# A two-layer graph network on one core: the constants are made and loaded in pieces between the first five turns

## The chip, the cores and the metric

The kernel runs on one core of one Trainium2 chip. The metric is the time of one execution on the device in microseconds (us). Times inside an execution come from one profiled run and count from the start of its span.

## The reference

64 graphs of 256 nodes with 256 features pass through two layers. Everything is computed in float32.

```
# layer 0
h = relu(layernorm(x));  A = adj + I;  d = rowsum(A) ** -0.5
x = x + relu((d A d) @ h @ W.T + b)
# layer 1, with the new x
h = relu(layernorm(x))
c = relu(bn1(conv1d(h, conv1_w, 1 tap)));  c = bn2(conv1d(c, conv2_w, 17 taps))
x_conv = relu(c + h)
s = h @ w_se.T + b_se;  D = exp(-|s_n - s_m|^2) * adj;  x_nmp = D @ relu(h @ w_msg.T + b_msg)
x = x + gru([x_conv, x_nmp], h)        # gates with w_ih, w_hh
```

bn(h) is h * g / sqrt(v + eps) + (b - m * g / sqrt(v + eps)). The scale of bn1 is multiplied into conv1_w, the scale of bn2 into the taps of conv2_w.

## The kernel before, in words

The program has three stages: the first runs over the 64 graphs (about 0 to 850 us), the second does the 17-tap convolution in the frequency domain, the third the gates. Only the start of the first stage is touched here.

The first stage is a software pipeline that is written out by hand. It has turns i = 0 to 71. In turn i every engine works on several graphs at once: graph i is loaded and its statistics are taken, graph i - 2 has its adjacency product (called AG here, with the graph's number), graph i - 3 its product with w0, graph i - 4 is transposed, graph i - 5 gets its products with wse and w1m, graph i - 6 its exponentials and graph i - 7 its Fourier transform and message product. Each engine has its own queue, with the functions first_sync, first_scalar, first_vector, first_gpsimd and first_tensor called for one turn after the other. Semaphores connect the queues, and an engine that waits holds up everything behind it in its queue. So turn 4 can be far along on DVE while TensorE is still at turn 3.

Each float32 product is done as three products of a high and a low part. ACT rounds the high part (names that end in h: ajh, hdxh, agh, w0h, w1mh, wseh), and DVE or GpSimd (POOL) subtracts it to get the low part (ajl, hdxl, agl, w0l, w1ml, wsel).

The constants: `ident` and `eye2` are unit matrices, `col` holds the per-channel vectors. From `col` DVE and GpSimd make `cold`, the scales and shifts of the two batch norms (with one power on GpSimd). DVE makes six diagonal matrices `diag` from it, TensorE multiplies them by ones so that each scale stands in a row in the banks CM1 and CM0 (the "rows"), ACT copies these to s1r, b1m and s2r. DVE multiplies st_w (the weights w1) by s1r, ACT and DVE split it in w1mh and w1ml. From s2r and the table tt_w DVE makes s2m and s2t, by which GpSimd scales the taps. `ft` and `gt` are the tables of the Fourier transforms.

In the kernel before, this whole chain stands on every engine between the calls for turn 3 and turn 4. ACT, GpSimd and DVE wait for its end before turn 4, and TensorE waits for s2r.

## Time and profile before

| | us |
|---|---|
| median of 3 runs | 1934.48 |
| lowest and highest | 1933.85, 1934.88 |
| the profiled execution, its own time | 1933.19 |
| its span | 1931.4 |
| TensorE busy | 1897.6 |
| DVE, ACT, GpSimd busy | 1118.9, 1029.9, 810.2 |

The profiled execution's own time is that of the whole program on the device; the span is the part that the trace shows. PE is TensorE, and PEld is its loading of weights. In a timeline row stand the start, the duration, the engine, the line of the kernel and the output and input names. In square brackets stands how long the engine was idle before it and what released it. Transfers are issued by the queue of SyncE (SP). Because matmuls overlap in the array, a row's duration is longer than the distance to the next row. The granted clock is given as a share of 2.4 GHz, so 0.50 is the level of 1.2 GHz.

### The profile page before, as it was taken

How to read it: one execution, taken by the hardware profiler on the slowest of the kernel's cores; microseconds unless marked ns; L12 is line 12 of the kernel's file. 1: busy time of each engine (PE TensorE's matmuls, PEld its weight loads, DVE VectorE, ACT ScalarE, POOL GpSimd, SP SyncE). 2: the span in 40 equal slices, each digit the busy share in tenths (PEclk: the TensorE clock that was granted, in tenths of full speed). 3: DMA queues.
4: the chain of work that ended last, by engine and by line, in shares of the span. 5: the costliest groups of instructions: out<-in, count | busy, mean ns of one | idle time of the engine just before them, and what ended most of it. 6: DMA issues, size and time to landing. Idle time of an engine off the chain costs nothing.

```text
span 1931.4 us, 29950 instructions
## 1 busy us (share of the span) xinstructions
PE 1897.6 (98%) x10524; PEld 1667.7 (86%) x10524; DVE 1118.9 (58%) x2187; ACT 1029.9 (53%) x1834; POOL 810.2 (42%) x1054
## 2 busy tenths in 40 slices
PE   4999999999999999999999999999999999999998
PEld 4899999999999989888888888888888888888887
DVE  6888989898887855444464344343344334434433
ACT  3888888888888875545563233233323323323322
POOL 4778888888776743333342122122122112212211
PEclk7999999999999999999999999999999999999999
DMA  5445655555455426556683322332232232233221
GB/s 170 158 169 177 212 189 195 180 193 200 171 201 182 148 99 157 143 138 163 147 224 108 115 91 92 104 108 84 95 115 86 86 115 86 87 114 97 87 96 55
DMA packets 254993, 262.58 MB, mean 136 GB/s; under 512 B 96519, under 2 KB 204423, under 8 KB 252798
## 3 DMA queue, kind: packets, MB, share of 16 engines
q1 hardware_dynamic: 254846, 260.68, 42.9%
q8 instruction: 85, 1.39, 0.3%
q14 instruction: 62, 0.51, 0.1%
HBM read 151.57 MB, written 109.05 MB: 135 GB/s over the span
## 4 chain that ended last, share of the span: by engine, by line
PE 96%; DVE 1%; ACT 1%; issue 1%; POOL 0%; DMA 0%; SPq 0%; DVEq 0%; POOLq 0%; ACTq 0%
PE P L104 77%; PE P L603 5%; PE P L872 5%; PE P L653 4%; PE P L632 3%; PE P L994 1%; PE P L624 1%; DMA yt<-y_d 0%; PE P L1265 0%; DVE ah L423 0%; DVE xxl L417 0%; POOL axl L534 0%; DVE wh0l L740 0%; DVE diag L1166 0%; ACT agh L344 0%
## 5 line engine op out<-in xcount | busy, mean ns | idle before, releaser
L856 POOL TENSOR_TENSOR xnx1l<-xnf,xnx1h 128x1024 fp32r<-128x1024 f32 x16 | 44.5, 2779 | 369.2 <-ACT xnx1h L849 369.2
L856 POOL TENSOR_TENSOR xnx0l<-xnf,xnx0h 128x1024 fp32r<-128x1024 f32 x15 | 41.6, 2773 | 340.4 <-ACT xnx0h L849 340.4
L967 DVE SCALAR_TENSOR_TENSOR gn<-tr,gn 128x512 f32<-128x512 f32 x64 | 44.3, 692 | 202.8 <-ACT tr L954 202.8
L954 ACT ACTIVATE tr<-P,cold 128x512 f32<-128x512 f32 x64 | 44.2, 690 | 217.1 <-PE P L104 217.1
L957 ACT ACTIVATE nn<-gn,col 128x512 f32<-128x512 f32 x64 | 46.3, 723 | 179.3 <-DVE gn L971 179.3
L534 POOL TENSOR_TENSOR axl<-af,axh 128x512 fp32r<-128x512 f32 x64 | 83.5, 1304 | 135.1 <-ACT axh L360 135.1
L961 ACT ACTIVATE tz<-P,cold 128x512 f32<-128x512 f32 x64 | 44.0, 688 | 164.0 <-PE P L104 164.0
L978 DVE SCALAR_TENSOR_TENSOR tz<-tz,tr 128x512 f32<-128x512 f32 x64 | 44.3, 692 | 149.7 <-ACT tz L961 149.7
L603 PE MATMUL P<-ft,h 128*128 128x240 f32 x512 | 114.3, 366 | 0.7 <-DVE x L444 0.7
L872 PEld LDWEIGHTS P<-gt,yt 128*128 128x128 f32 x768 | 108.3, 191 | 5.6 <-DMA yt<-y_d 0.8
L104 PE MATMUL P<-w1mh,xxh 128*128 128x512 f32 x256 | 112.1, 438 | 0.0
L872 PE MATMUL P<-gt,yt 128*128 128x128 f32 (+2 forms) x768 | 105.7, 287 | 0.2
L104 PE MATMUL P<-w1mh,xxl 128*128 128x512 f32 x256 | 101.2, 395 | 0.0
L104 PE MATMUL P<-w1ml,xxh 128*128 128x512 f32 x256 | 101.1, 395 | 0.0
L603 PEld LDWEIGHTS P<-ft,h 128*128 128x128 f32 x512 | 92.5, 190 | 5.8 <-issue 0.8
L971 DVE TENSOR_TENSOR gn<-gn,P 128x512 f32<-128x512 f32 x64 | 44.0, 688 | 86.7 <-PE P L104 86.6
L104 PE MATMUL P<-w0h,agh 128*128 128x256 f32 x256 | 85.2, 333 | 5.0 <-DVE w0l L1150 3.0
L104 PE MATMUL P<-ajh,hdxh 128*128 128x256 f32 x256 | 74.3, 290 | 14.5 <-DVE hdxl L402 12.4
L325 ACT ACTIVATE msh<-tcm 128x512 fp32r<-128x512 f32 x64 | 40.5, 632 | 89.5 <-PE P L104 88.7
L495 DVE TENSOR_TENSOR tcm<-P,b1m 128x512 f32<-128x512 f32 x64 | 44.2, 691 | 74.5 <-ACT h L382 74.5
L531 POOL TENSOR_TENSOR af<-af,at 128x512 f32<-128x512 f32 x64 | 82.2, 1284 | 7.3 <-ACT af L319 7.3
L539 POOL TENSOR_TENSOR ajl<-ah,ajh 128x512 fp32r<-128x512 f32 x64 | 82.2, 1285 | 2.0 <-ACT ajh L339 2.0
(219 smaller groups left out, 6710.0 us busy)
## 6 DMA issues: line engine op xcount, KB each, us to landing
xh_d<-xst SPq DMA_DIRECT2D x16, 1280.0 KB, 7.2
xl<-xh_d SPq DMA_DIRECT2D x40, 512.0 KB, 6.2
y_d<-yo SPq DMA_DIRECT2D x80, 256.0 KB, 2.4
x<-in_x SPq DMA_DIRECT2D x64, 256.0 KB, 3.0
a<-in_adj SPq DMA_DIRECT2D x64, 256.0 KB, 4.4
at<-in_adjt SPq DMA_DIRECT2D x64, 256.0 KB, 4.8
x_d<-x SPq DMA_DIRECT2D x64, 256.0 KB, 4.8
xn_d<-xt SPq DMA_DIRECT2D x64, 256.0 KB, 5.1
```

The source lines that it names most:

```text
L104: done = e.matmul(o, l, r, start=start, stop=stop, skip_group_check=True)
L531: e.e.tensor_tensor(af[:, :], af[:, :], at[b % 7][:, :], ALU.mult).then_inc(S["am"], 1)
L534: e.e.tensor_tensor(ax[1][:, :], af[:, :], ax[0][:, :], ALU.subtract).then_inc(S["axlo"], 1)
L539: e.e.tensor_tensor(ajl[b % 2][:, :], ah[:, :], ajh[b % 2][:, :], ALU.subtract).then_inc(S["ajlo"], 1)
L603: t = e.e.matmul(P[k][:, 0:3 * NT] if n == 0 else P[k][:, NT:4 * NT], h1[b % 2][:, n, c * 128:c * 128 + 128], ft[:, NT:4 * NT] if n == 0 e ...
L632: t = e.e.matmul(P[DIST][:, m * 256:m * 256 + 256], uv[0:96, 0, m * 128:m * 128 + 128], uv[0:96, 1, :], start=True, stop=True, skip_group_ ...
L653: t = e.e.matmul(P[k][:, m * 140:m * 140 + 140], taps[0:n_rows, j0 + m, c * 128:c * 128 + 128], tt_w[0:n_rows, part * 140:part * 140 + 140 ...
L856: e.e.tensor_tensor(o[1][:, :, :], xnf[p % 2][:, :, :, :].rearrange("p c i t -> p c (i t)"), o[0][:, :, :], ALU.subtract).then_inc(done, 1)
L872: t = e.e.matmul(P[k][:, o * 256 + first:o * 256 + last], y[:, j, o * 128:o * 128 + 128], gt[:, g:g + last - first], start=j == 0, stop=j ...
L957: e.e.activation(nn[:, :], gn[:, :], ACT.Tanh, bias=n_b[:, o:o + 1]).then_inc(S["nn"], 1)
L967: e.e.scalar_tensor_tensor(out=gn[:, :], in0=tr[:, :], scalar=1.0, in1=gn[:, :], op0=ALU.add, op1=ALU.mult).then_inc(S["v"], 1)
L978: e.e.scalar_tensor_tensor(out=tz[:, :], in0=tz[:, :], scalar=1.0, in1=tr[:, :], op0=ALU.add, op1=ALU.mult).then_inc(S["e"], 1)
```

## The change

The operations and the transfers are all kept. Their places in the queues change:

- SyncE: x, adj and the transposed adj of graph 0 come first, then eye2, col and ident, then x and adj of graph 1. tt_w is loaded after turn 4's loads, ft after turn 5's, gt after turn 20's.
- DVE: the first step of cold comes after turn 0; the rest of it and diag after turn 1; w0l and the scaling of st_w after turn 2; w1ml and wsel after turn 3; s2m, s2t and the two memsets of uv after turn 4.
- GpSimd: the power comes ahead of turn 0.
- TensorE: the rows' matmuls come after turn 2 (that is, behind AG0) and no longer after turn 3.
- ACT: w0h comes after turn 1, s1r and b1m after turn 2, w1mh, wseh and s2r after turn 3.
- The wait for all constants on ACT, GpSimd and DVE comes after turn 4, not after turn 3.

```diff
         def first_sync(e, i):
             if live(i, 0):
-                if i == 0:
-                    load_x(e, 0)
-                    load_adj(e, 0)
...
@@ sync
+            load_x(e, 0)
+            load_adj(e, 0)
+            load_adjt(e, 0)
+            sync.dma_start(eye2[:, :], eye).then_inc(S["eye2_in"], 16)
+            sync.dma_start(col[:, 0:29], cols).then_inc(S["col_in"], 16)
             sync.dma_start(ident[:, :], eye[:, 0:128]).then_inc(S["ident_in"], 16)
-            first_sync(e, 0)
-            sync.dma_start(col[:, 0:29], cols).then_inc(S["col_in"], 16)
-            sync.dma_start(eye2[:, :], eye).then_inc(S["eye2_in"], 16)
+            load_x(e, 1)
+            load_adj(e, 1)
             first_sync(e, 1)
...
             first_sync(e, 3)
+            first_sync(e, 4)
+            sync.dma_start(tt_w[:, :], ttab).then_inc(S["tt_in"], 16)
+            first_sync(e, 5)
             sync.dma_start(ft[:, :], ftab).then_inc(S["ft_in"], 16)
-            sync.dma_start(gt[:, :], gtab).then_inc(S["gt_in"], 16)
-            sync.dma_start(tt_w[:, :], ttab).then_inc(S["tt_in"], 16)
-            for i in range(4, TURNS):
+            for i in range(6, TURNS):
                 first_sync(e, i)
+                if i == 20:
+                    sync.dma_start(gt[:, :], gtab).then_inc(S["gt_in"], 16)
@@ scalar
-            for i in range(3):
+            for i in range(2):
                 first_scalar(e, i)
             e.wait_ge(S["w0_in"], 16)
             scalar.copy(w0[0][:, :, :], st_w0[:, :, :]).then_inc(S["chi"], 1)
-            first_scalar(e, 3)
+            first_scalar(e, 2)
             e.wait_ge(S["rows"], 1)
             scalar.copy(s1r[:, :], P[CM1][:, 0:256])
-            scalar.copy(b1m[:, 0:256], P[CM1][:, 256:512])
-            e.wait_ge(S["rows"], 2)
-            scalar.copy(s2r[:, 0:256], P[CM0][:, 0:256])
-            scalar.copy(s2r[:, 256:7 * NW], P[CM0][:, 0:7 * NW - 256]).then_inc(S["normrow"], 2)
+            scalar.copy(b1m[:, 0:256], P[CM1][:, 256:512]).then_inc(S["normrow"], 1)
+            first_scalar(e, 3)
             e.wait_ge(S["w1s"], 1)
             scalar.copy(w1m[0][:, :, :], st_w1[:, :, :]).then_inc(S["chi"], 1)
             e.wait_ge(S["se_in"], 16)
             scalar.copy(wse[0][:, :, :], st_se[:, :, :]).then_inc(S["chi"], 1)
+            e.wait_ge(S["rows"], 2)
+            scalar.copy(s2r[:, 0:256], P[CM0][:, 0:256])
+            scalar.copy(s2r[:, 256:7 * NW], P[CM0][:, 0:7 * NW - 256]).then_inc(S["normrow"], 1)
+            first_scalar(e, 4)
             e.wait_ge(S["clo"], 3)
             e.wait_ge(S["s2t"], 2)
-            for i in range(4, TURNS):
+            for i in range(5, TURNS):
                 first_scalar(e, i)
@@ gpsimd
-            for i in range(4):
-                first_gpsimd(e, i)
             e.wait_ge(S["consts"], 1)
             gpsimd.tensor_tensor(cold[:, 0:4], cold[:, 20:24], half[:, 0:4], ALU.pow).then_inc(S["crs"], 1)
+            for i in range(5):
+                first_gpsimd(e, i)
@@ tensor
-            for i in range(4):
+            for i in range(3):
                 first_tensor(e, i)
...
             t.then_inc(S["rows"], 1)
+            for i in range(3, 5):
+                first_tensor(e, i)
             e.wait_ge(S["normrow"], 2)
-            for i in range(4, TURNS):
+            for i in range(5, TURNS):
                 first_tensor(e, i)
```

Three places in the queues, as they stand in the program. First TensorE at turns 2 and 3, where the rows' matmuls (P<-diag,ones) now stand behind the last matmul of AG0 and ahead of the first product with w0:

```order
 L104 MATMUL P<-ajl_77,hdxh 128x256
 L104 MATMUL P<-ajh_75,hdxl 128x256
+L1275 MATMUL P<-diag,ones 128x128 [waits one,diag]
+L1275 MATMUL P<-diag,ones 128x128 x3
+L1279 MATMUL P<-diag,ones 128x128 x2
 L104 MATMUL P<-w0h,agh 128x256 [waits clo,aglo,aghi]
 L104 MATMUL P<-w0l,agh 128x256
```

The rows moved up by one turn; before, they stood behind AG1.

Second ACT at the start, where hd is the normalised graph and w0h a constant. Before:

```order
L374 ACTIVATE hd<-x_81,sm_100 128x256 [waits sbias]
L374 ACTIVATE hd<-x_81,sm_100 128x256
L307 CAST hdxh<-hd 128x512 [waits hd]
L339 CAST ajh_76<-ah 128x512 [waits ah]
L344 CAST agh<-P 128x512 [waits agg]
L374 ACTIVATE hd<-x_82,sm_101 128x256 [waits hdlo,sbias]
L374 ACTIVATE hd<-x_82,sm_101 128x256
L1088 CAST w0h<-st_w_122 128x512 [waits w0_in]
```

And now:

```order
L371 ACTIVATE hd<-x_81,sm_100 128x256 [waits sbias]
L371 ACTIVATE hd<-x_81,sm_100 128x256
L1092 CAST w0h<-st_w_122 128x512 [waits w0_in]
L304 CAST hdxh<-hd 128x512 [waits hd]
L336 CAST ajh_76<-ah 128x512 [waits ah]
L341 CAST agh<-P 128x512 [waits agg]
```

The copy w0h, which waits for the load of w0, moved ahead of hdxh of graph 0.

Third ACT between turns 3 and 4, behind hd of graph 2, as it is now:

```order
L371 ACTIVATE hd<-x_83,sm_102 128x256 [waits hdlo,sbias]
L371 ACTIVATE hd<-x_83,sm_102 128x256
L1099 CAST w1mh<-st_w_123 128x1024 [waits w1s]
L1101 CAST wseh<-st_se 128x256 [waits se_in]
L1103 COPY s2r<-P 128x256 [waits rows]
L1104 COPY s2r<-P 128x3
L304 CAST hdxh<-hd 128x512 [waits hd]
```

Before, s1r and b1m stood here too, and hdxh waited for all of the constants (its row had [waits hd,s2t,clo]).

## Rows read from the trace of the kernel before

**Rows 1.** The page: busy time of TensorE, and its chain.

```profile
PE 1897.6 (98%) x10524; PEld 1667.7 (86%) x10524; DVE 1118.9 (58%) x2187; ACT 1029.9 (53%) x1834; POOL 810.2 (42%) x1054
PE 96%; DVE 1%; ACT 1%; issue 1%; POOL 0%; DMA 0%; SPq 0%; DVEq 0%; POOLq 0%; ACTq 0%
```

**Rows 2.** Windows: stretch, length, busy us (instructions) by engine, clock, DMA, GB/s.

```profile
24.00:29.00 5.00, 0.00 (x0) 0.00 (x0) 3.56 (x20) 1.18 (x3) 1.01 (x1) 0.76 0.69 211
29.00:47.00 18.00, 13.79 (x59) 12.86 (x60) 13.90 (x34) 9.22 (x19) 7.80 (x19) 0.50 0.20 58
48.00:66.00 18.00, 17.45 (x117) 15.49 (x115) 15.24 (x39) 16.34 (x32) 12.50 (x22) 1.00 0.46 148
66.00:850.00 784.00, 782.04 (x5008) 718.14 (x5009) 614.22 (x1379) 625.07 (x1211) 536.25 (x839) 1.00 0.54 173
```

**Rows 3.** Timeline of TensorE in the first 50 us.

```profile
12.40 0.55 PE L104 MATMUL P<-ajh,hdxh 128*128 128x256 f32 x1 [12.40 <-DVE hdxl L402]
...
14.89 0.41 PE L104 MATMUL P<-ajh,hdxl 128*128 128x256 f32 x1
18.30 0.55 PE L104 MATMUL P<-w0h,agh 128*128 128x256 f32 x1 [2.99 <-DVE w0l L1150]
...
23.29 0.28 PE L104 MATMUL P<-ajh,hdxl 128*128 128x256 f32 x1
29.16 2.08 PE L1265 MATMUL P<-diag,ones 128*128 128x128 f32 x8 [5.59 <-DVE diag L1166]
31.02 1.06 PE L1269 MATMUL P<-diag,ones 128*128 128x128 f32 x4
...
45.52 0.41 PE L104 MATMUL P<-ajh,hdxh 128*128 128x256 f32 x1
```

**Rows 4.** Timeline of DVE in the first 53 us.

```profile
11.57 0.73 DVE L402 TENSOR_TENSOR hdxl<-hd,hdxh 128x512 fp32r<-128x512 f32 x1
...
25.49 0.36 DVE L394 BATCH_NORM_AGGREGATE sm<-sm 128x2 f32<-128x6 f32 x4
...
27.84 1.26 DVE L1166 TENSOR_SCALAR diag<-ident,cold 128x128 f32<-128x128 f32 x6
...
33.27 0.42 DVE L1174 TENSOR_TENSOR s2m<-s2r,tt_w 119x259 f32<-119x259 f32 x1
...
36.80 0.69 DVE L402 TENSOR_TENSOR hdxl<-hd,hdxh 128x512 fp32r<-128x512 f32 x1
...
40.16 1.29 DVE L454 TENSOR_SCALAR sm<-sm 128x2 f32<-128x2 f32 x1
...
43.58 0.66 DVE L402 TENSOR_TENSOR hdxl<-hd,hdxh 128x512 fp32r<-128x512 f32 x1
...
52.93 0.69 DVE L402 TENSOR_TENSOR hdxl<-hd,hdxh 128x512 fp32r<-128x512 f32 x1 [2.25 <-ACT hdxh L307]
```

**Rows 5.** SyncE's queue: the issue of w0's load; then loads, us to landing.

```profile
6.53 0.47 SPq L1030 DMA_DIRECT2D st_w<-in_w0t x1
...
st_w<-in_w0t SPq DMA_DIRECT2D x1, 256.0 KB, 5.2
st_w<-in_w1mt SPq DMA_DIRECT2D x1, 512.0 KB, 6.2
```

**Rows 6.** Timeline of ACT in the first 35 us.

```profile
16.82 0.61 ACT L1088 CAST w0h<-st_w 128x512 fp32r<-128x512 f32 x1
...
24.09 1.09 ACT L374 ACTIVATE hd<-x,sm 128x256 f32<-128x256 f32 x2
...
33.39 1.04 ACT L1097 CAST w1mh<-st_w 128x1024 fp32r<-128x1024 f32 x1 [0.83 <-DVE st_w L1171]
```

**Rows 7.** Timeline of GpSimd between turns 3 and 4.

```profile
25.99 1.01 POOL L1236 TENSOR_TENSOR cold<-cold,half 128x4 f32<-128x4 f32 x1 [4.63 <-DVE cold L1153]
```

**Rows 8.** The chain that ended last: start, length, what.

```profile
42.82 5.02 PE P L104 x24
...
72.06 4.97 PE P L104 x42
```

More of the change, by code:

```diff
@@ L1146, in _ @@
             e = Engine(vector)
-            for i in range(3):
-                first_vector(e, i)
-            e.wait_ge(S["chi"], 1)
-            vector.tensor_tensor(w0[1][:, :, :], st_w0[:, :, :], w0[0][:, :, :], ALU.subtract).then_inc(S["clo"], 1)
-            first_vector(e, 3)
+            first_vector(e, 0)
             e.wait_ge(S["col_in"], 16)
             vector.tensor_scalar(cold[:, 20:24], col[:, 12:16], EPS, None, ALU.add).then_inc(S["consts"], 1)
+            first_vector(e, 1)
             e.wait_ge(S["crs"], 1)
@@ L1160, in _ @@
             vector.tensor_tensor(cold[:, 8:12], col[:, 16:20], col[:, 22:26], ALU.add).then_inc(S["consts"], 1)
+            e.wait_ge(S["ident_in"], 16)
             e.wait_ge(S["consts"], 5)
-            vector.tensor_scalar(cold[:, 8:12], cold[:, 8:12], 0.5, None, ALU.mult)
-            vector.tensor_scalar(cold[:, 12:14], col[:, 26:28], 0.5, None, ALU.mult)
-            e.wait_ge(S["ident_in"], 16)
             for n, k in enumerate((0, 1, 4, 5, 2, 3)):
@@ L1167, in _ @@
             t.then_inc(S["diag"], 1)
-            e.wait_ge(S["normrow"], 2)
+            vector.tensor_scalar(cold[:, 8:12], cold[:, 8:12], 0.5, None, ALU.mult)
+            vector.tensor_scalar(cold[:, 12:14], col[:, 26:28], 0.5, None, ALU.mult)
+            first_vector(e, 2)
+            e.wait_ge(S["chi"], 1)
+            vector.tensor_tensor(w0[1][:, :, :], st_w0[:, :, :], w0[0][:, :, :], ALU.subtract).then_inc(S["clo"], 1)
+            e.wait_ge(S["normrow"], 1)
             e.wait_ge(S["w1_in"], 16)
@@ L1172, in _ @@
             t.then_inc(S["w1s"], 1)
+            first_vector(e, 3)
+            e.wait_ge(S["chi"], 2)
+            vector.tensor_tensor(w1m[1][:, :, :], st_w1[:, :, :], w1m[0][:, :, :], ALU.subtract).then_inc(S["clo"], 1)
+            e.wait_ge(S["chi"], 3)
+            vector.tensor_tensor(wse[1][:, :, :], st_se[:, :, :], wse[0][:, :, :], ALU.subtract).then_inc(S["clo"], 1)
+            first_vector(e, 4)
+            e.wait_ge(S["normrow"], 2)
             e.wait_ge(S["tt_in"], 16)
@@ L1177, in _ @@
             vector.tensor_reduce(s2t[:, :], s2m[:, :, :], AX_X, ALU.add).then_inc(S["s2t"], 1)
-            e.wait_ge(S["chi"], 2)
-            vector.tensor_tensor(w1m[1][:, :, :], st_w1[:, :, :], w1m[0][:, :, :], ALU.subtract).then_inc(S["clo"], 1)
-            e.wait_ge(S["chi"], 3)
-            vector.tensor_tensor(wse[1][:, :, :], st_se[:, :, :], wse[0][:, :, :], ALU.subtract).then_inc(S["clo"], 1)
             e.wait_ge(S["clo"], 3)
@@ L1232, in _ @@
             e.wait_ge(S["half"], 1)
-            for i in range(4):
-                first_gpsimd(e, i)
             e.wait_ge(S["consts"], 1)
             gpsimd.tensor_tensor(cold[:, 0:4], cold[:, 20:24], half[:, 0:4], ALU.pow).then_inc(S["crs"], 1)
+            for i in range(5):
+                first_gpsimd(e, i)
             e.wait_ge(S["clo"], 3)
             e.wait_ge(S["s2t"], 2)
-            for i in range(4, TURNS):
+            for i in range(5, TURNS):
                 first_gpsimd(e, i)
@@ L1271, in _ @@
             t.then_inc(S["rows"], 1)
+            for i in range(3, 5):
+                first_tensor(e, i)
             e.wait_ge(S["normrow"], 2)
-            for i in range(4, TURNS):
+            for i in range(5, TURNS):
                 first_tensor(e, i)
```

## The prediction

> **What bounds the kernel now.** I read the page first. TensorE is busy for 98% of the span, and 96% of the chain that ended last is TensorE's [rows 1]. So only what makes TensorE wait, or run slowly, can move the time. The windows say where that is: from 66 to 850 us it is busy for 782.04 of 784 us, from 24 to 29 us for 0.00 of 5, and from 29 to 47 us for 13.79 of 18 with a granted clock of 0.50, which is the 1.2 GHz level [rows 2]. The constants are made in just that stretch.
>
> The start of TensorE's timeline shows the same. The first group of 12 matmuls (the adjacency product of graph 0, "AG0") begins at 12.40 and ends near 15.3. The first product with w0 begins at 18.30 after 2.99 us of idle time, released by w0l. The last matmul of AG1 begins at 23.29. Then come 5.59 us of nothing until diag is there at 29.16, and AG3 begins only at 45.52 [rows 3]. On DVE the normal work of turn 3 ends at 25.8 and that of turn 4 begins at 36.80. The 11.0 us between hold the chain cold, diag, rows, s1r, w1mh, w1ml, and every queue waits for its end [rows 4]. DVE then begins turn 5 at 43.58 and turn 6 at 52.93 [rows 4]. I use these starts as checkpoints: how much earlier does each come after the change? Once TensorE has no gaps, a lead is kept to the end, since the clock stands at 1.00 and nearly nothing waits from 66 us on [rows 2].
>
> **The change, part by part.** No instruction is added or removed, so the sum is made of waits.
>
> (1) *The head, a loss of 1.3 us.* On ACT the copy w0h now stands ahead of hdxh of graph 0. It waits for the w0 load, issued at 6.53 and 5.2 us on its way, so there at 11.7 [rows 5]. The same loads (nine of 256 KB, cols and ident) are asked for ahead of it in either order, so I leave 11.7. Then w0h takes 0.61 [rows 6], hdxh about as much, ready near 12.9, and from hdxl's start to AG0's it was 0.83 (11.57 to 12.40, [rows 3, 4]). AG0 begins at 13.7 instead of 12.40. The bounds are 0 (the copy fits before hd is ready) and 2 us (the load lands 0.7 later).
> The power on GpSimd, 1.01 us [rows 7], now runs ahead of graph 0's statistics, but needs only the cols load; it delays hd by little, as hd stood behind ajh before. DVE makes cold and diag (2.1 us, from the end of the power at 27.0 to the last diag near 29.1, [rows 4, 7]) while it would wait for hdxh. Both costs lie under the w0 wait.
>
> (2) *The rows' matmuls, no cost.* They take 2.9 us (29.16 to 32.08, [rows 3]) and stand between AG0 and the first w0 product, where TensorE idled 2.99 us. AG0 ends at 16.6, the rows at 19.5. The w0 product begins there instead of at 18.30: 1.2 us late. Without the gap they would cost 2.9.
>
> (3) *Turn 3.* Everything follows the w0 product by the same distances as before, so DVE's last row of turn 3 ends at 27.0, or 26.3 if only AG1's own end counts; I take 26.7 (before 25.8). The st_w product and s1r's copies are done while AG1's inputs are late anyway.
>
> (4) *From turn 3 to turn 5, the gain.* ACT's hd of graph 2 began at 24.09 and took 1.0 [rows 6]; 0.9 later it ends at 26.0, and w1mh (1.04) at 27.05. So DVE waits 0.35 us where 11.0 stood. The rest of the constants' DVE work stays: from 33.27 to 36.80 it took 3.5 us [rows 4], now split in w1ml and wsel ahead of turn 4 and s2m, s2t and the memsets behind it. ACT's wseh and s2r are smaller than w1mh, together 0.9 at most, so with them hdxh is begun by 28.0 and ready near 28.5, when DVE is through w1ml and wsel (a little under half of the 3.5, so near 28.6). They cost nothing, but only just. Turn 4 itself took 43.58 - 36.80 = 6.8. Turn 5 begins at 26.7 + 0.35 + 3.5 + 6.8 = 37.4 instead of 43.58: a lead of 6.2. Of turn 4's time 1.1 went to a single tiny operation of DVE that took 1.29 at 40.16 [rows 4]; without it the lead is 7.3. I take 6.8.
>
> (5) *Turn 5 and the clock.* In the kernel before, the clock was 0.50 until 47 us [rows 2]. From DVE's start of turn 5 to AG3's it was 1.94 us (43.58 to 45.52), as the product ahead still ran at the low level. With only hdxl in the way it is 0.83, so 1.1 less. At the high level 42 matmuls of 256 columns take 4.97, or 0.118 each; at the low one 24 take 5.02 from 42.82 on, or 0.209 each [rows 8]. AG3 at the high level is then up to 0.9 shorter (12 x 0.09 is 1.1, but its last part had the high level before). Together 2.0, and DVE's idle time ahead of turn 6, 2.25 us with hdxh to blame [rows 4], is there to be saved. So if the clock is up in turn 5, the lead grows by 1.1 to 2.0, I take 1.6: 6.8 + 1.6 = 8.4. If it is down all through it, the six small and twelve 512-column matmuls that had the high level before cost 6 x 0.09 = 0.5 and 12 x 0.18 = 2.2 more, and AG3 0.2: 2.9 less the 1.1 is a loss of 1.8, and nearer 0 if the clock rises halfway.
>
> The clock came back only when TensorE had worked without a gap from 42.82 to 47 us [rows 8], and was lost in the gap of 5.59 us: the window from 24 to 29 us, all of it idle, has 0.76 on average, so the fall comes well inside the idle stretch [rows 2, 3]. After the change no single gap is that long. The longest I find are about 2 us, ahead of AG2 and of the next two products, with TensorE busy for somewhat under half of the time between 25 and 36 us. I take it that the clock rises during AG1 as before and stays.
> The Trainium skill speaks against this: "TensorE: Matmul & The Clock Gate", section "A second HAM failure mode: psum-queue depth-cycling", has TensorE idling briefly but often between groups of matmuls, and its clock going up and down from that. By that rule the gain would be that of the low clock below, 6.0 us; no run here yet shows which holds.
>
> (6) *The loads.* x1 and a1 now come behind eye2, cols and ident: some 0.4 MB more ahead of them, about 1 us at the pace of this stretch, hidden by DVE's other work. tt_w is issued only after a load that waits for x2 of graph 0 (near 24.7), so at 26.6, and needs 6.2 us if it is as slow as the slowest load of that time [rows 5]: there at 32.8, wanted by DVE near 34. ft is wanted only in turn 7, gt after the first stage. Nothing is lost, with 1 us to spare for tt_w.
>
> **The sum.** -8.4 us against the profiled execution's own 1933.19 (its span is 1931.4) gives 1924.8. The median of the runs is 1934.48, 1.3 above it, so the forecast is 1926.1.
>
> **The rivals.**
> *A, the clock falls between turns 3 and 5.* For it: TensorE works less than half of that time. Against it: the only fall in the trace came in one long gap. Lead 6.8 plus between -1.8 (low all through turn 5) and +0.2 (up again right behind AG3, so that only AG3 and the small ones pay), so -0.8: 6.0 us gained, 1928.5; down to 6.2 - 1.8 = 4.4 with the smaller lead, 1930.1.
> *B, the pieces land on queues that were not idle.* DVE and ACT are busy 13.90 and 9.22 us of the 18 from 29 to 47 us. If w1mh, wseh and s2r hold up hdxh, and with it AG2, agh and the next product, by their full 1.9 us, the head costs 2 instead of 1.3, and the clock is low too, then 4.4 - 1.9 - 0.7 = 1.8 us are left: 1932.7, within 0.2%. That asks for three things at once.
> *C, slower: the late tt_w load.* DVE's s2m waits for it, and s2t holds all of turn 5 on ACT, GpSimd and DVE. Each us beyond 34 costs one. It decides if the load takes over 8.4 + 7.4 = 15.8 us from its issue; at 20 us the kernel would take 1938.7. The slowest early load took 6.2 [rows 5], which speaks against it.
> *D, more than forecast.* w0 lands before hd is ready (0.6 less loss), no slow operation (7.3) and the full 2.0: 9.9, or 1924.6; up to 11, or 1923.5, if the turns also lose small waits.
>
> **How the numbers follow.** Forecast (clock stays up) 0.52, A 0.28, B 0.08, C 0.03, D 0.09. The range takes in the forecast, A with its smaller lead, and D: 1923.5 to 1930.4, which leaves about 0.14 out. 0.2% is 3.9 us, about what a measurement of this kernel can tell from no change. Forecast, A and D gain more: 0.88 with a hundredth off for overlap. B, with the small end of A, is the same: 0.09. C: 0.03.
>
> **What would show it.** In the changed kernel's profile: AG0 near 13.7, released behind w0h; the rows' matmuls straight behind AG0 with no gap ahead of the w0 product; DVE's turn 4 starting near 28.6, turn 5 near 36.8 and turn 6 near 44.5 (before 36.80, 43.58, 52.93); granted clock 1.00 between 25 and 45 us. A clock of 0.50 in turn 5 shows A; DVE waiting ahead of s2m for a DMA shows C; ACT's w1mh beginning after 27 us, or hdxh of graph 2 after 29, shows B. From turn 7 on both kernels should need the same time for a turn; if they don't, the prediction is wrong in its ground.

## The result, and the profile after

| | median us | lowest to highest, runs |
|---|---|---|
| before | 1934.16 | 1932.19 to 1934.88, 4 |
| changed | 1922.36 | 1921.82 to 1923.34, 4 |

The ratio is 0.9941, with a 95% interval of 0.9924 to 0.9958. The change gains 11.8 us. The forecast was 8.4, so 1926.1, with a range that began at 1923.5. The time lies 1.1 us below it. The profiled execution took 1921.82 us, with a span of 1920.0. When the same kernel was measured once more with the last experiments (the run *again*), it had 1923.75 (1922.47 to 1924.92, 5 runs) beside 1933.6 for the kernel before (1932.58 to 1935.41, 9 runs), which is 9.85 gained. That median would lie just inside the forecast's range, so a median of a few runs is good to about 1 us here, and the 1.1 us alone prove little. The traces are clearer: both profiled executions of the changed kernel have more than the 8.4 us of the forecast (11.9 and 11.0 us at the first Fourier product), and the part that failed can be named.

The page of the changed kernel, busy time and the chain that ended last (compare [rows 1]):

```profile
PE 1890.4 (98%) x10524; PEld 1660.9 (87%) x10524; DVE 1117.7 (58%) x2187; ACT 1029.5 (54%) x1834; POOL 811.3 (42%) x1054
PE 97%; DVE 1%; ACT 1%; issue 1%; DMA 0%; POOL 0%; SPq 0%; DVEq 0%; POOLq 0%; ACTq 0%
```

TensorE still bounds the kernel, with the same 10524 matmuls. They are busy for 7.2 us less, as fewer of them run at the low level.

The windows of the changed kernel, with the columns and stretches of [rows 2]:

```profile
24.00:29.00 5.00, 3.31 (x24) 2.96 (x24) 5.00 (x15) 2.52 (x8) 3.67 (x7) 1.00 0.75 244
29.00:47.00 18.00, 14.78 (x96) 13.21 (x97) 17.00 (x48) 15.12 (x30) 11.99 (x27) 1.00 0.51 162
48.00:66.00 18.00, 17.43 (x121) 16.31 (x121) 16.60 (x42) 15.24 (x30) 15.13 (x26) 1.00 0.51 167
66.00:850.00 784.00, 782.13 (x4998) 717.51 (x4997) 609.29 (x1362) 622.47 (x1203) 529.77 (x826) 1.00 0.54 173
```

Where TensorE did nothing from 24 to 29 us it now does 24 matmuls, and from 29 to 47 us it does 96 and not 59, at the high level. DVE, busy for only 58% of the span, is the one to look at: 5.00 of 5 us and 17.00 of 18. While the pipeline fills, DVE sets the pace and TensorE has time to spare.

TensorE's timeline of the changed kernel, as [rows 3]:

```profile
13.54 0.55 PE L104 MATMUL P<-ajh,hdxh 128*128 128x256 f32 x1 [13.54 <-DVE hdxl L399]
...
16.02 0.41 PE L104 MATMUL P<-ajh,hdxl 128*128 128x256 f32 x1
16.24 1.27 PE L1275 MATMUL P<-diag,ones 128*128 128x128 f32 x8
17.35 0.61 PE L1279 MATMUL P<-diag,ones 128*128 128x128 f32 x4
18.66 0.36 PE L104 MATMUL P<-w0h,agh 128*128 128x256 f32 x1 [0.70 <-DVE w0l L1174]
18.86 0.28 PE L104 MATMUL P<-w0l,agh 128*128 128x256 f32 x1
18.97 0.28 PE L104 MATMUL P<-w0h,agl 128*128 128x256 f32 x1
...
24.18 0.36 PE L104 MATMUL P<-w0h,agh 128*128 128x256 f32 x1 [2.43 <-DVE agl L470]
...
31.42 0.35 PE L104 MATMUL P<-w0h,agh 128*128 128x256 f32 x1 [1.69 <-DVE agl L470]
...
34.51 0.36 PE L104 MATMUL P<-ajh,hdxh 128*128 128x256 f32 x1 [1.45 <-ACT hdxh L304]
...
54.18 1.86 PE L600 MATMUL P<-ft,h 128*128 128x240 f32 x8 [0.57 <-DVE x L441]
```

The rows' matmuls stand behind AG0 without a gap, as forecast. But they take 1.7 us and not the 2.9 of [rows 3]: the last four take 0.61 where four took 1.06. The first w0 product then runs with 0.12 us from start to start, the high level, where AG0 ran with 0.21. The clock rose early in the rows' matmuls, near 16.5 us (an estimate: from 16.24 the first eight take 1.11 us up to the next row; they took 1.86 at the low level, and 0.99 in c_both below, all at the high one). The first Fourier product begins at 54.18; before it was 66.10. That is a lead of 11.9 us, of which 11.4 are left in the span. From turn 8 (60.45 for 72.37) to turn 65 (670.86 for 682.64) on DVE the lead goes from 11.92 to 11.78 us, so both kernels need the same time per turn within 0.01 us; the other 0.4 goes behind that, where the change touches nothing.

The kernel was profiled a second time (again), and there the clock rose later:

```profile
16.93 1.91 PE L1275 MATMUL P<-diag,ones 128*128 128x128 f32 x8
18.64 1.06 PE L1279 MATMUL P<-diag,ones 128*128 128x128 f32 x4
19.36 0.55 PE L104 MATMUL P<-w0h,agh 128*128 128x256 f32 x1
...
20.35 0.28 PE L104 MATMUL P<-w0l,agh 128*128 128x256 f32 x1
```

All the rows' matmuls ran at the low level here, and the high one came near 20.3 us, inside the first w0 product. What that product's start has to do with the level is taken up in step 2 below.

DVE's timeline of the changed kernel, as [rows 4]:

```profile
10.22 2.28 DVE L1168 TENSOR_SCALAR diag<-ident,cold 128x128 f32<-128x128 f32 x6
...
12.74 0.69 DVE L399 TENSOR_TENSOR hdxl<-hd,hdxh 128x512 fp32r<-128x512 f32 x1
...
19.30 0.68 DVE L399 TENSOR_TENSOR hdxl<-hd,hdxh 128x512 fp32r<-128x512 f32 x1
...
24.66 0.36 DVE L391 BATCH_NORM_AGGREGATE sm<-sm 128x2 f32<-128x6 f32 x4
24.93 1.19 DVE L1182 TENSOR_TENSOR w1ml<-st_w,w1mh 128x1024 fp32r<-128x1024 f32 x1
26.04 0.42 DVE L1184 TENSOR_TENSOR wsel<-st_se,wseh 128x256 fp32r<-128x256 f32 x1
26.38 0.69 DVE L399 TENSOR_TENSOR hdxl<-hd,hdxh 128x512 fp32r<-128x512 f32 x1
...
29.81 0.16 DVE L452 TENSOR_SCALAR sm<-sm 128x2 f32<-128x2 f32 x1
29.88 0.68 DVE L458 SCALAR_TENSOR_TENSOR x<-x,x 128x512 f32<-128x512 f32 x1
...
32.02 0.40 DVE L1188 TENSOR_TENSOR s2m<-s2r,tt_w 119x259 f32<-119x259 f32 x1
...
33.72 0.69 DVE L399 TENSOR_TENSOR hdxl<-hd,hdxh 128x512 fp32r<-128x512 f32 x1
...
41.30 0.69 DVE L399 TENSOR_TENSOR hdxl<-hd,hdxh 128x512 fp32r<-128x512 f32 x1 [0.56 <-ACT hdxh L304]
...
50.10 0.69 DVE L399 TENSOR_TENSOR hdxl<-hd,hdxh 128x512 fp32r<-128x512 f32 x1 [0.34 <-ACT hdxh L304]
```

Each hdxl begins a turn. None of these rows from 12.74 to 33.72 has a wait in brackets, the pieces of the constants included. Against [rows 4] turn 4 begins 10.4 us earlier (26.38 for 36.80), turn 5 9.9 (33.72 for 43.58), turn 6 11.6 (41.30 for 52.93) and turn 7 11.9 (50.10 for 62.02).

ACT's timeline of the changed kernel, as [rows 6]:

```profile
10.59 1.09 ACT L371 ACTIVATE hd<-x,sm 128x256 f32<-128x256 f32 x2 [2.54 <-POOL sm L523]
11.59 0.60 ACT L1092 CAST w0h<-st_w 128x512 fp32r<-128x512 f32 x1
12.10 0.61 ACT L304 CAST hdxh<-hd 128x512 fp32r<-128x512 f32 x1
...
23.26 1.03 ACT L1099 CAST w1mh<-st_w 128x1024 fp32r<-128x1024 f32 x1
```

And GpSimd's, as [rows 7]:

```profile
6.95 1.33 POOL L1244 TENSOR_TENSOR cold<-cold,half 128x4 f32<-128x4 f32 x1 [5.91 <-DVE cold L1156]
...
29.90 0.71 POOL L523 TENSOR_TENSOR sm<-sm 128x2 f32<-128x2 f32 x1
30.58 1.27 POOL L536 TENSOR_TENSOR ajl<-ah,ajh 128x512 fp32r<-128x512 f32 x1
```

At the head the queue was held in another place than forecast. hd waited for GpSimd, which first waited for cold and then ran the power: the statistics of graph 0 began behind it at 8.25 us. w0h then ran without a wait for its load, and hdxl stood behind diag. This differs between executions of the same kernel: in again hd began at 10.80, and w0h at 12.28 after 0.39 us of waiting for its load, and hdxl then waited 0.60 us for hdxh.

### The profile page after: what moved, and what is told of

The parts are those of the page before. It is cut to its first block, busy times and chain, and to the rows that moved or that the text cites. A ratio compares the mean times of both kernels' runs of the same rounds, so it can differ in the third digit from the quotient of the medians.

```text
span 1920.0 us, 29952 instructions
## 1 busy us (share of the span) xinstructions
PE 1890.4 (98%) x10524; PEld 1660.9 (87%) x10524; DVE 1117.7 (58%) x2187; ACT 1029.5 (54%) x1834; POOL 811.3 (42%) x1054
## 4 chain that ended last, share of the span: by engine, by line
PE 97%; DVE 1%; ACT 1%; issue 1%; DMA 0%; POOL 0%; SPq 0%; DVEq 0%; POOLq 0%; ACTq 0%
PE P L104 77%; PE P L600 5%; PE P L869 5%; PE P L650 4%; PE P L629 3%; PE P L991 2%; PE P L621 1%; DMA col<-in_cols 0%; ACT hd L371 0%; DMA yt<-y_d 0%; DVE x L441 0%; ACT hdxh L304 0%; DVE sm L430 0%; DVE ah L420 0%; DVE hdxl L399 0%
```

## The experiments

The checkpoints are those above: the start of AG0, the turns on DVE, and the first Fourier product. The experiments ran in three groups. The kernel before, measured in each group, had 1933.02 (25 runs), 1933.01 (9) and 1933.6 (9). Ratios are to it. Where AG0 begins is not exact to a tenth: the four profiled kernels with the head of the kernel before (before, c_gap, c_hole, c_both) have 12.40, 13.13, 12.64 and 12.15, and the five with the head of the changed one (changed, again, late, x_act, x_dve) have 13.54, 14.24, 14.04, 14.17 and 13.92.

**First group: what the clock is worth, and what the long wait is worth.** Three kernels take the kernel before and only keep TensorE busy. The extra products go to a bank that is overwritten later. *c_gap* fills the idle stretch behind AG0, as the rows' matmuls do in the changed kernel:

```diff
-            for i in range(4):
+            for i in range(3):
                 first_tensor(e, i)
+            e.wait_ge(S["one"], 1)
+            for n in range(6):
+                tensor.matmul(P[DFT][:, 0:128], ones[:, :], ones[:, :], start=True, stop=True, skip_group_check=True)
+            first_tensor(e, 3)
```

> The kernel before, with six extra 128x128 float32 matmuls of ones in TensorE's idle time between AG0 and the first w0 product (into a bank that nothing uses yet). My theory now: in the changed kernel the rows' matmuls fill this gap, the clock therefore rises near 17 us instead of 23, and turn 3 ends 1.8 us early from that. Then here too the matmuls of the w0 product stand about 0.12 us apart, DVE's last row of turn 3 ends near 24.2 instead of 25.8, and the kernel takes 1.5 to 2 us less than the kernel before. Rival: the early rise comes from something else (the phase of whatever the chip looks at); then the clock still rises near 23 us and the time is that of the kernel before, within 0.5 us.

*c_hole* fills the 5.59 us behind AG1 in which the clock fell:

```diff
             for i in range(4):
                 first_tensor(e, i)
+            for n in range(44):
+                tensor.matmul(P[DFT][:, 0:256], w0[0][:, 0, 0:128], w0[0][:, 0, :], start=True, stop=True, skip_group_check=True)
```

> The kernel before, with 44 extra 128x256 matmuls behind AG1, 5.2 us of work in the idle time of 5.6 us ahead of the rows. The chain of constants is untouched. Theory: the clock then stays up from 23 us on, which saves about 1.3 us on the rows, little in turn 4 (DVE and ACT set its pace), and about 2 in turn 5: 3 to 4 us less than the kernel before, so the clock is about a third of the 11.8 us and the stall of the queues the rest. Rival: the gain of the change is mostly the clock; then this kernel gains 7 us or more.

*c_both* has both edits.

> The kernel before with both fillers, so that TensorE's clock is up from 17 us on and the chain of constants stands where it stood. Theory: the two gains add, 5 to 6 us less than the kernel before, and 6 us stay for the move of the chain itself. Rival (clock is nearly all): 10 us or more.

| | median us (range, runs) | ratio (95%) | first Fourier product |
|---|---|---|---|
| c_gap | 1930.94 (1929.56 to 1932.93, 10) | 0.999 (0.998 to 0.9999) | 62.98 |
| c_hole | 1931.40 (1930.23 to 1932.35, 10) | 0.9991 (0.9981 to 1.0001) | 63.43 |
| c_both | 1930.37 (1928.58 to 1931.94, 10) | 0.9986 (0.9977 to 0.9996) | 62.62 |

The first w0 product on TensorE in c_gap:

```profile
19.02 0.36 PE L104 MATMUL P<-w0h,agh 128*128 128x256 f32 x1 [1.58 <-DVE w0l L1150]
19.22 0.28 PE L104 MATMUL P<-w0l,agh 128*128 128x256 f32 x1
19.34 0.28 PE L104 MATMUL P<-w0h,agl 128*128 128x256 f32 x1
```

And the last row of turn 3 on DVE in c_gap:

```profile
24.21 0.37 DVE L394 BATCH_NORM_AGGREGATE sm<-sm 128x2 f32<-128x6 f32 x4
```

Six small matmuls in the gap bring the w0 product and AG1 to 0.12 us from start to start. Turn 3, from its hdxl at 18.79 to this row, takes 5.42 us. In the kernel before it took 7.42 (18.07 to 25.49). In the changed kernel it takes 5.36 (19.30 to 24.66). In c_hole, with no filler in the gap, turn 3 and the chain behind it keep their length: 10.95 us from hdxl to the rows' matmuls, before 11.09, c_gap and c_both 9.09. So the early clock alone is enough for the 2 us of turn 3. It takes them out of two waits, which DVE has in turn 3 of the kernel before and in c_gap no more:

```profile
21.24 0.88 DVE L444 SCALAR_TENSOR_TENSOR x<-P,sm,b 128x256 f32<-128x256 f32 x2 [1.22 <-PE P L104]
...
24.22 0.69 DVE L473 TENSOR_TENSOR agl<-P,agh 128x512 fp32r<-128x512 f32 x1 [0.65 <-ACT agh L344]
```

In the changed kernel the clock had help. There the first w0 product begins 0.64 us before turn 3's hdxl (18.66 and 19.30), before it began 0.23 behind it (18.30 and 18.07), so DVE would have waited less at either level. An estimate: with the distances of the kernel before from the w0 product on (2.94 us to x, 5.92 to agl), DVE would have waited 0.4 us at x and 0.75 at agl. So some 1.2 of the 2 us are the clock there, and 0.9 the earlier product. In again, where the clock rose only near 20.3 us, turn 3 took the same 5.36 us, with the product 0.88 us ahead of hdxl. No run took the clock's rise out of the changed kernel, so this division is not shown.

The second thing that the group tells is a limit. Both fillers together gained 2.65 us, and I had expected about twice that; c_hole gained 1.6 for an expected 3 to 4, and its interval still takes in no gain at all. One window of c_both shows why:

```profile
29.00:47.00 18.00, 13.09 (x68) 12.13 (x69) 17.11 (x44) 10.79 (x22) 10.44 (x24) 0.72 0.28 87
```

The clock fell again, in the 3.31 us in which TensorE waited for hdxh of turn 4, and turn 5 was slow once more (9.37 us from hdxl to hdxl, before 9.35). In c_hole it fell in turn 4 too (0.60 from 36 to 40 us), behind a wait as long. By c_hole and c_gap, in which the clock was back in time, turn 5 is 7.95 and 7.85 long.

The lead of 11.9 us that the changed kernel has on DVE at turn 7 can now be added up. Turn 3 is 2.1 us shorter, turn 4 1.1 (the slow operation of [rows 4] is not there), turn 5 1.8 and turn 6 0.3. The long wait behind turn 3 went from 11.31 us (25.49 to 36.80) to 1.72 (24.66 to 26.38), with 1.70 more behind turn 4, so it gives 7.9. The later hdxl of turn 3 (19.30 for 18.07) takes 1.2 back. Of the 7.9, the high level alone gives back 1.2: from hdxl of turn 3 to that of turn 4 it is 16.73 us in c_gap and 15.51 in c_both. The rest, near 6.7, came back in none of the kernels in which only the clock was helped.

**Is it the place of the pieces, or only that they are pieces?** *late* takes the changed kernel and moves the pieces between turns 3 and 4 behind turn 4, on ACT and DVE:

```diff
 @@ scalar, behind first_scalar(e, 3)
+            first_scalar(e, 4)
             e.wait_ge(S["w1s"], 1)
             scalar.copy(w1m[0][:, :, :], st_w1[:, :, :]).then_inc(S["chi"], 1)
...
             scalar.copy(s2r[:, 256:7 * NW], P[CM0][:, 0:7 * NW - 256]).then_inc(S["normrow"], 1)
-            first_scalar(e, 4)
 @@ vector, behind first_vector(e, 3)
+            first_vector(e, 4)
             e.wait_ge(S["chi"], 2)
             vector.tensor_tensor(w1m[1][:, :, :], st_w1[:, :, :], w1m[0][:, :, :], ALU.subtract).then_inc(S["clo"], 1)
...
-            first_vector(e, 4)
```

> The changed kernel, with w1mh, wseh, s2r (ACT) and w1ml, wsel (DVE) moved from behind turn 3 to behind turn 4, together with s2m and s2t. Theory: between 25 and 41 us DVE is busy nearly all the time, so the place of its constants in the queue matters little and their sum counts: the time is that of the changed kernel, 0 to 1.5 us more, since now ACT's 1.6 us and DVE's 3.2 us come one behind the other with DVE waiting for w1mh. DVE's turn 4 starts 1.5 us earlier, its turn 5 0 to 1.5 later. Rival: the spreading over several turns is what gains; then a block in one place costs 3 us or more.

Measured 1925.56 (1923.90 to 1926.67, 4 runs), ratio 0.9962 (0.9947 to 0.9977), first Fourier product 56.66. The Fourier product is 2.5 us behind that of the changed kernel and 1.5 behind that of again; late gains 7.5 us over the kernel before beside it, where the changed kernel gained 9.9 and 11.8, and its profiled execution is the fastest of its four. It falls between the two expectations. The wait that I had overlooked stands on TensorE, in the row of late where turn 5 begins with its product with w0:

```profile
33.67 0.58 PE L104 MATMUL P<-w0h,agh 128*128 128x256 f32 x1 [3.78 <-ACT s2r L1105]
34.05 0.42 PE L104 MATMUL P<-w0l,agh 128*128 128x256 f32 x1
```

TensorE waits for both copies to be out of the banks before turn 5, and the copy s2r came late; 3.78 us of idle time also cost the high level (0.21 from start to start behind it). So some of the long wait comes back if these pieces are put in one place, even one turn later, and the place counts for some 1.5 to 4 us.

**Second group: the head.** Three kernels try to take away the 1.1 us (1.8 in again) by which AG0 is late. *v1* puts w0h behind hdxh of graph 0. *v2* puts GpSimd's power behind the statistics of turns 0 and 1, and DVE's cold and diag behind hdxl of graph 0. *v3* does both. The function given as third argument is called right behind hdxh or hdxl; round_w0 and make_diag hold the lines that are taken out.

```diff
 @@ v1, scalar
-            e.wait_ge(S["w0_in"], 16)
-            scalar.copy(w0[0][:, :, :], st_w0[:, :, :]).then_inc(S["chi"], 1)
-            first_scalar(e, 2)
+            first_scalar(e, 2, round_w0)
 @@ v2, gpsimd
+            for i in range(2):
+                first_gpsimd(e, i)
             e.wait_ge(S["consts"], 1)
             gpsimd.tensor_tensor(cold[:, 0:4], cold[:, 20:24], half[:, 0:4], ALU.pow).then_inc(S["crs"], 1)
-            for i in range(5):
+            for i in range(2, 5):
                 first_gpsimd(e, i)
 @@ v2, vector
-            e.wait_ge(S["crs"], 1)
-            vector.tensor_tensor(cold[:, 0:4], cold[:, 0:4], col[:, 0:4], ALU.mult).then_inc(S["consts"], 1)
...
-            first_vector(e, 2)
+            first_vector(e, 2, make_diag)
```

> The changed kernel with the copy w0h put behind hdxh of graph 0 (ahead of ajh of graph 1). Theory: in the changed kernel's trace hd of graph 0 waits 2.54 us for GpSimd and w0h runs right behind it without waiting for its load, so w0h costs only its own 0.5 us; but DVE is busy with diag till 12.6, so hdxl cannot start before that and the time stays the same within 0.3 us. Rival (my prediction): the w0 load sets AG0's start; then AG0 begins at 12.9 or earlier and the kernel gains 0.6 to 1.2 us.

> The changed kernel with the power on GpSimd put behind turn 1 (behind graph 0's statistics and ajl) and DVE's cold and diag put behind hdxl of graph 0. Theory: graph 0's statistics are 1.3 us earlier, hd starts near 8.3 instead of 10.59, DVE is free for hdxl; w0h still stands ahead of hdxh and its load lands near 11.4, so now the load does set the start: AG0 near 13.2 instead of 13.54, the kernel 0 to 0.5 us faster.

> Both moves together: hd near 8.3, hdxh near 9.3, hdxl near 10, AG0 near 10.8 instead of 13.54. Theory: nothing else holds AG0, and the loads of graph 1 come in time, so the kernel is 2 to 2.7 us faster than the changed kernel, 13.8 to 14.5 faster than the kernel before. Rival: the loads (x, adj of graphs 1 to 3, w0) set the pace of turns 2 and 3; then the lead at AG0 is given back by AG1 and the time is that of the changed kernel within 0.5 us.

*u_sp* is the changed kernel with the loads in the order of the kernel before:

```diff
-            load_x(e, 0)
-            load_adj(e, 0)
-            load_adjt(e, 0)
-            sync.dma_start(eye2[:, :], eye).then_inc(S["eye2_in"], 16)
-            sync.dma_start(col[:, 0:29], cols).then_inc(S["col_in"], 16)
             sync.dma_start(ident[:, :], eye[:, 0:128]).then_inc(S["ident_in"], 16)
+            load_x(e, 0)
+            load_adj(e, 0)
             load_x(e, 1)
             load_adj(e, 1)
+            load_adjt(e, 0)
+            sync.dma_start(col[:, 0:29], cols).then_inc(S["col_in"], 16)
+            sync.dma_start(eye2[:, :], eye).then_inc(S["eye2_in"], 16)
```

> The changed kernel with the load order of the kernel before (ident first, cols and eye2 behind graph 1's loads, ft, gt and tt_w behind turn 3's). Theory: cols then lands near 7.7 instead of 6.6, so the power, graph 0's statistics behind it and hd are 1.1 us later, eye2 lands near 8.5 and ah with it: AG0 near 14.7, the kernel 1 to 1.3 us slower than the changed kernel. The late tables make no difference. Rival: the load order is worth nothing (the w0 load lands at the same time in both); then AG0 stays at 13.5 and the time is the same.

| | median us (range, 5 runs) | ratio (95%) | AG0 | first Fourier product |
|---|---|---|---|---|
| v1 | 1922.19 (1921.06 to 1922.32) | 0.9943 (0.993 to 0.9955) | 13.86 | 54.64 |
| v2 | 1922.74 (1921.91 to 1923.38) | 0.9947 (0.9935 to 0.996) | 13.76 | 55.18 |
| v3 | 1920.39 (1919.05 to 1923.78) | 0.9937 (0.9924 to 0.9951) | 11.45 | 53.22 |
| u_sp | 1923.24 (1922.88 to 1923.48) | 0.9949 (0.9937 to 0.9962) | 15.05 | 55.93 |

Neither v1 nor v2 alone moves AG0 out of the 13.54 to 14.24 us that the same head has elsewhere: it is held in two places, and each takes over when the other is gone. In v1 GpSimd's power still holds hd; in v2 w0h now waits for its load and holds hdxh (hdxl at 12.96 after 2.84 us of idle time, released by hdxh). Both edits together bring AG0 to 11.45, 2.1 us earlier than in the changed kernel and 2.8 earlier than in again. But only 1.0 and 1.9 us of it reach the first Fourier product. DVE has hardly any idle time from 10.65 on in v3 (3.89, 4.00, 3.97 and 4.00 us busy in the four stretches of 4 us from 12 on), and diag, which has left the stretch ahead of hdxl, now stands behind it (12.07 to 13.3). A head that is earlier is paid back by the engine that sets the pace. In this execution the clock fell as well. TensorE's timeline of v3:

```profile
22.99 0.36 PE L104 MATMUL P<-w0h,agh 128*128 128x256 f32 x1 [2.26 <-DVE agl L472]
...
23.65 0.41 PE L104 MATMUL P<-w0h,agl 128*128 128x256 f32 x1
23.86 0.42 PE L104 MATMUL P<-w0h,agh 128*128 128x256 f32 x1
```

From 23.65 on a matmul of 256 columns stands 0.21 us from the next. The granted clock is 0.50 from 24 to 28 us and 0.69 to 32. Turn 4's and turn 5's DVE times hardly show it (7.58 us each; the changed kernel has 7.34 and 7.58), because TensorE does not set the pace there.

u_sp shows what the new order of the loads does. With the old order AG0 comes 1.2 to 1.5 us later than in v1 and the changed kernel (0.8 later than in again), and the time is 1.05 us longer than that of v1 and 0.5 longer than that of v2 beside it. It is the constants' loads that matter: DVE's first step of cold waits for cols until 8.36, where it was 6.62, and GpSimd's power and all behind it move with it. From hdxl of turn 3 to that of turn 5 u_sp takes 14.43 us, the changed kernel 14.42. The loads act on the head alone.

**Third group: which engine sets the pace.** *x_dve* puts one more subtraction of 1024 columns ahead of w1ml on DVE, *x_act* one more copy of 1024 columns ahead of w1mh on ACT. Both write to xst, a buffer that is filled later:

```diff
 @@ x_dve, vector
             e.wait_ge(S["chi"], 2)
+            vector.tensor_tensor(xst[0][:, 0, 0:64, :].rearrange("p r t -> p (r t)"), st_w1[:, :, :].rearrange("p k n -> p (k n)"), w1m[0][:, :, :].rearrange("p k n -> p (k n)"), ALU.subtract)
             vector.tensor_tensor(w1m[1][:, :, :], st_w1[:, :, :], w1m[0][:, :, :], ALU.subtract).then_inc(S["clo"], 1)
 @@ x_act, scalar
             e.wait_ge(S["w1s"], 1)
+            scalar.copy(xst[0][:, 0, 0:64, :].rearrange("p r t -> p (r t)"), st_w1[:, :, :].rearrange("p k n -> p (k n)"))
             scalar.copy(w1m[0][:, :, :], st_w1[:, :, :]).then_inc(S["chi"], 1)
```

> The changed kernel with one more DVE subtraction of 128x1024 (some 1.2 us) ahead of w1ml, into a tile that nothing uses yet. Theory: from hdxl of graph 0 on DVE has no idle time until turn 6, and its queue sets the pace of turns 3 to 5, so 1.0 to 1.2 us come out at the end: turn 4 starts near 27.6 instead of 26.38, and the kernel is 1.0 to 1.2 us slower than the changed kernel of the same job. Rival: TensorE's waits or ACT set the pace; then 0 to 0.3.

> The changed kernel with one more ACT copy of 128x1024 (1.0 us) ahead of w1mh. Theory: ACT had w1mh ready 0.75 us before DVE came to it, and hdxh of graph 2 1.0 us before, so of the 1.0 us only 0.2 to 0.3 come out. Rival (B of the prediction: the pieces on ACT hold up hdxh and with it everything): 1.0 us.

*again* is the changed kernel itself, as the measure for this group:

> The changed kernel itself, for the three above to stand against on the same chip: 1922.4 within 0.5 us, 11 to 12 us less than the kernel before.

*v4* is v3 with the wait for the constants in turn 5 moved behind hdxh on ACT and, with the two memsets of uv, behind hdxl on DVE:

```diff
 @@ scalar
-            e.wait_ge(S["clo"], 3)
-            e.wait_ge(S["s2t"], 2)
-            for i in range(5, TURNS):
+            first_scalar(e, 5, constants_done)
+            for i in range(6, TURNS):
 @@ vector
-            e.wait_ge(S["clo"], 3)
-            e.wait_ge(S["s2t"], 2)
-            vector.memset(uv[32:64, 0, :], -0.5)
-            vector.memset(uv[64:96, 1, :], -0.5).then_inc(S["ones"], 1)
-            for i in range(5, TURNS):
+            first_vector(e, 5, fill_uv)
+            for i in range(6, TURNS):
```

> The kernel v3 (w0h behind hdxh of graph 0, the power behind turn 1, cold and diag behind hdxl of graph 0) and in addition in turn 5: hdxh of graph 3 on ACT and hdxl on DVE stand ahead of the wait for the constants and of the two memsets of uv. Theory: AG3 starts 0.6 us earlier, and TensorE's unbroken stretch from AG3 to the transposes of graph 1, which releases turn 6, with it: 0.5 to 0.6 us less than v3, so some 2.5 us less than the changed kernel of the same job. Rival: DVE's sum of work is what counts up to turn 6, and then the order of these few changes nothing: like v3.

| | median us (range, 5 runs) | ratio (95%) | turn 3 to turn 5 on DVE | first Fourier product |
|---|---|---|---|---|
| again | 1923.75 (1922.47 to 1924.92) | 0.9948 (0.9935 to 0.996) | 20.24 to 34.66 = 14.42 | 55.12 |
| x_dve | 1924.05 (1923.19 to 1927.28) | 0.9955 (0.9942 to 0.9967) | 19.85 to 36.54 = 16.69 | 59.25 |
| x_act | 1924.99 (1923.90 to 1925.66) | 0.9956 (0.9942 to 0.9969) | 19.95 to 35.85 = 15.90 | 56.29 |
| v4 | 1921.61 (1920.11 to 1923.97) | 0.9940 (0.9927 to 0.9952) | | 52.61 |

again came out 1.3 us above what was expected of it. By the medians alone x_dve missed its 1.0 to 1.2 us: they would have said that 1.1 us more on DVE costs 0.3, and as much on ACT 1.2, and the ranges overlap. The traces tell more. From hdxl of turn 3 to that of turn 4, the stretch in which the extra operation stands, again takes 7.09 us, x_dve 8.22 and x_act 7.48. So there DVE's 1.1 us is paid in full, and ACT's copy with 0.4. What comes behind is less simple. Three of x_dve's five runs lie at 1923.2 to 1924.1, two at 1926.7 and 1927.3, and the profiled execution is the last of these. Two windows of it:

```profile
24.00:29.00 5.00, 2.76 (x13) 2.52 (x14) 5.00 (x13) 1.99 (x5) 3.20 (x4) 0.61 0.68 194
29.00:40.00 11.00, 8.01 (x40) 7.54 (x41) 10.63 (x28) 6.50 (x12) 7.22 (x19) 0.66 0.50 167
```

This is rival A of the prediction, in single executions: the clock down in turns 4 and 5, and turn 5 with 9.73 us (36.54 to 46.27) where it has 7.59 in again. It costs 2.1 us there.

In x_act the copy itself costs 0.3 to 0.4: DVE's w1ml waited 0.26 us for w1mh. ACT had room, as expected. The other 1.1 us is one instruction of turn 4 on DVE:

```profile
30.78 0.17 DVE L451 TENSOR_SCALAR sm<-sm 128x2 f32<-128x2 f32 x1
30.86 1.25 DVE L452 TENSOR_SCALAR sm<-sm 128x2 f32<-128x2 f32 x1
32.02 0.68 DVE L458 SCALAR_TENSOR_TENSOR x<-x,x 128x512 f32<-128x512 f32 x1
```

And on GpSimd in x_act at that time:

```profile
30.78 1.30 POOL L536 TENSOR_TENSOR ajl<-ah,ajh 128x512 fp32r<-128x512 f32 x1
```

The tiny operation takes 1.25 us beside GpSimd's subtraction, which began 0.08 us ahead of it, and ends with it. In the changed kernel the same operation took 0.16 at 29.81. There DVE's x<-x,x began first, at 29.88, and a tiny operation of GpSimd at 29.90 took 0.71 instead of 0.2 and let ajl start only at 30.58. The slow operation of [rows 4] at 40.16 is of the same kind, beside an ajl that began at 40.16. In x_dve it was x<-x,x (1.77 us at 31.61, not 0.68, beside an ajl from 31.56); that and its own 1.1 us make the 2.3 by which turn 5 comes later there. So a tenth of a microsecond in who begins first decides over 1.1 us on the engine that sets the pace. This is no chance of the single execution: the slow operation stands in turn 4 in all four profiled kernels that keep the old chain (before, c_gap, c_hole, c_both), and in none of changed, again, v1, v2 and u_sp, whose turn 4 has the same rows as the changed kernel's. The order of the queues decides it, by a margin that is easily lost, and 1.1 us of the change's gain hang on it.
The Trainium skill, "SBUF — State Buffer", section "SBUF: two separate sides", says that VectorE and GpSimd share a pair of ports as an exclusive lock, and that whichever begins first keeps it for its whole instruction; VectorE needs the pair for an operation with two inputs in SBUF (against a GpSimd operation that reads SBUF) or in a mode that uses both ports. These rows agree with the lock in both directions (1.25 us on DVE, 0.71 on GpSimd); that the tiny operation, with its one input, ran in such a mode is not shown.

v3 and v4 are the fastest, 0.6% ahead of the kernel before. By the medians v4 is 2.1 us ahead of again beside it and v3 1.8 ahead of v1 beside it; the ranges overlap, so that they beat the changed kernel is likely and not shown. v3 and v4 are not told apart: v4's first Fourier product comes 0.6 us earlier, but 0.4 of that is there at AG0 (11.04 for 11.45), where its edit does nothing yet.

## Why the prediction was wrong, step by step

**What bounds it**: right, with a gap. That only TensorE's waits count, and that a lead is kept once it has no gaps, held: 11.9 us at the first Fourier product, 11.4 in the span. But I looked for TensorE's gaps and did not name the engine that makes them while the pipeline fills. It is DVE, with 22.0 of 23 us busy between 24 and 47 us. Once that is said, steps 3 to 5 are sums over DVE's queue.

**Step 1**, a loss of 1.3 us: the size was right (AG0 at 13.54, a loss of 1.14; 1.84 in again), the mechanism half wrong. The power, which was to "delay hd by little", made the statistics of graph 0 begin at 8.25 us, where they began at 6.14 before and at 5.53 in v3: GpSimd waited for cold until 6.95 and then ran the power for 1.33 us, and hd waited for it. The load of w0 held nothing in the profiled execution of the changed kernel, but in again and late w0h waited 0.39 and 0.35 us for it. v1 and v2 show that either place alone gives the same head, v3 that both must go. That the sum came out right is partly luck.

**Step 2**, the rows' matmuls in the gap: right in kind, 0.7 us too dear. The w0 product came 0.4 us late (18.66 for 18.30) and not 1.2. That is not the clock: it stands 5.12 us behind the start of AG0 both here and in again, where all of the filler ran at the low level, and I had 5.8. I had counted AG0 and the rows with 2.9 us each, to the end of their last matmul; from start to start it is 2.7 and, in again, 2.4.

**Step 3** is the step that failed: "Everything follows the w0 product by the same distances as before, so DVE's last row of turn 3 ends at 27.0", taken as 26.7. It ended at 24.94, 1.8 us earlier: 0.8 of that the earlier w0 product, the rest the distance behind it. The distances of before were those of the low level, with DVE waiting 1.22 and 0.65 us for TensorE and for what follows it. With the gap filled the clock rose before AG1 and not near its end (near 16.5 us, near 20.3 in again, before 23.1), both waits were gone, and turn 3 was 2 us shorter: from hdxl on DVE's own work was its length. c_gap repeats this in the kernel before with nothing else changed, so it is shown that the filler's clock can do it alone; in the changed kernel the earlier w0 product had a share, by the estimate above. I had asked of the filler what it costs, and of the clock whether it would fall, and never whether the filler would raise it.

**Step 4**, the gain between turns 3 and 5: mechanism right, size 1.3 us short. The wait of 0.35 for w1mh did not come, as all of turn 3 was early. The constants took 1.45 and 1.70 us, 3.15 and not 3.5. Turn 4 took 5.64 (26.38 to 32.02); I had used 6.2, halfway between with and without the slow operation, and it was without. That was no middle to be taken: by the traces the operation is slow in every kernel with the old chain and fast in every one with the changed kernel's order, and x_act shows that a small shift brings its 1.1 us back. Turn 5 began at 33.72 and not at 36.8.

**Step 5**, the clock in turn 5: right where it stayed up. Turn 5 took 7.58 us for 9.35 before, 1.8 less; I took 1.6. That the clock "rises during AG1 as before" was wrong, it rose ahead of it. That it stays up held in the profiled executions of the changed kernel, again, v2 and u_sp. In those of v1, v3, v4, x_act and x_dve it fell for part of the stretch from 20 to 40 us, and in late behind the gap of 3.78 us. Where it fell in the executions without a profile is not on record, so how often it stays up isn't known, and that it did in the profiled one is partly luck. A small misreading in the sum: the 0.209 us for the low level was a mean over 24 matmuls of which the last five stand closer; the others stand 0.213 apart. It changes less than 0.1 us.
The rule of the Trainium skill that I had set against this step ("TensorE: Matmul & The Clock Gate", section "A second HAM failure mode: psum-queue depth-cycling") has such falls and rises with short gaps. They came in five of the ten profiled kernels with pieces, but in neither execution of the changed kernel, where the granted clock was 1.00 throughout.

**Step 6**, the loads: tt_w was there when wanted, and s2m began at 32.02 without a wait. That the other moved loads cost nothing was too modest: their order gives about 1 us at the head (u_sp: AG0 0.8 to 1.5 us later without it), as col comes earlier.

**The rivals.** A is real in single executions, at 2.1 us in x_dve's turn 5. B did not come: w1mh began at 23.26 and hdxh of graph 2 at 24.82. C did not come. D, more than forecast, is what happened, but by a term that it did not have: the forecast's 8.4, plus 1.75 from turn 3, 1.3 from step 4, 0.2 from step 5 and 0.3 from turn 6 (8.80 us, before 9.09) make the 11.9 of the first Fourier product. The range ended at 11.0 gained, and that end was made of waits alone, with nothing for a clock that rises earlier. The last sign named, that from turn 7 on both kernels need the same time for a turn, held.
